# Moving a step's attention scores ahead of the next slot, and its Q and K transposes ahead of the previous step's values, in the transformer half of a Taylor-attention plus transformer kernel

## Chip, cores and metric

The kernel runs on one core of one Trainium2 chip. The metric is the device time of the whole kernel in microseconds (us). Engines: PE is TensorE (matmuls; PEld its weight loads), DVE is VectorE, ACT is ScalarE, POOL is GpSimd, SP is SyncE, which here only issues DMAs.

## What is computed

The input x is (8, 1024, 256), float32. It is layer-normalised to `xn`, and the result is `x + attention(xn) + ffn(xn)`:

```python
x = L0_attn_hidden_states
xn = _layernorm(x, axis=-1)
x = x + _L0_attn_ref(xn, ...) + _L0_ffn_ref(xn, ...)
```

The first branch is a linear attention with a Taylor feature map. The change doesn't touch it. The second branch is a transformer of two layers (DEPTH = 2) with 8 heads of 64, a local window of 128 tokens and a gated feed-forward part:

```python
h = shift_token(x)
q, k, v = jnp.split(h @ wqkv, 3, axis=-1)
q = l2norm(q) * qs; k = l2norm(k) * ksc
q, k = rotary_xpos(q, k)
o = local_attention(q, k, v)      # this block of 128 keys and the one before, masked softmax
x = x + o @ wo
h = shift_token(x)
h = (h - mu) / jnp.sqrt(var + 1e-05) * lg + lb
a, g = jnp.split(h @ w1 + b1, 2, axis=-1)
x = x + (a * gelu(g)) @ w2 + b2
```

## The kernel before, in words

`taylor_block` (lines up to 653) computes `xn` and the linear attention and leaves both in DRAM. Then `transformer_block` runs the two layers and adds everything up. All that follows is about `transformer_block`.

Work is cut into **steps**. A step is one tile of 128 tokens in one layer, `(n, s, l, it)`: its number n, the stream s (the batch is split into two streams), the layer l and the tile it of the stream. There are 4 x 32 = 128 steps. Time is cut into **slots**. In slot j every engine runs its own function `slot(nxt, cur, att, nrm, ffn)`, and five steps are in it at five stages:

- `nxt` (step of slot j+1): its input tile is transposed (`x_T`, lines 1319 and 1320) and copied to `hT` by ACT.
- `cur`: Q, K and V projections (`project`, line 1327, bank by bank), copies of K and Q to `qk` by ACT (line 1213), squares (1221), norms and rotation on DVE and POOL, and at the end of the slot the transposes of K and Q (`heads_T`, line 1332), which ACT copies to `kT` and `qT` (1235 and 1240).
- `att`: scores (`scores`, lines 1352 for the middle and 1359 for the corners of a band), mask and row maximum on DVE (1079, 1086), exponentials on ACT (1246), division on DVE (1096), transposes of the probabilities (`prob_T`, 1370 and 1374), the product with the values (`attend`, lines 1389 for the middle and 1399 for the corners), copy to `oT` by ACT (1259), and the output projection (`out_project`, 1408).
- `nrm`: residual add on DVE (`add_attention`, 1108), statistics (1113 and, of the shifted half `xsh`, 1115), reciprocal root on POOL (973), normalisation (1125, 1126), transposes (`hn_T`, 1415) and copy to `hnT` by DVE (1132).
- `ffn`: up projection and gate (`up`, 1431 and 1436), GELU on ACT (1268, 1271), product on DVE (1142), down projection (`down`, 1443), last add (1149 or 1155).

The order of the work is written out by hand: each engine's `slot` is a fixed list, the same in every slot, with semaphore waits between engines. An engine that waits holds up everything behind it. From slot 7 to slot 127 all five stages are filled, except that a few slots at the two ends miss one.

On DVE the list begins with `add_attention(nrm)`, which needs the output projection that is PE's last work of the slot before. Then come the four `mask_scores(att, p)`, the statistics, `normalise`, the rotations of K, the gate, the norm and rotations of Q, and `unit_k(cur)` (line 1069), which scales K by its norm and signals `k_unit`. `heads_T` of K waits for `k_unit`. Behind `unit_k` stand `add_ffn`, `set_mask(nxt)` and `copy_hnT(nrm)`.

On SP the list begins with `shift(nrm)` (lines 888 and 889), which waits for `x1_ready` of `add_attention` and moves half of the tile down by one row (`xsh`), for the second statistics. Behind it are `keep_k` (894), `carry` (914), `load_residual` (882, 883; it waits for `xb_ready` of POOL's `residual`, line 1007, and runs where l is 1), `place_v` (906, 907) and `keep_v` (899 to 901).

PSUM has 8 banks, and this table says who uses which:

```python
SCORES = (0, 1, 2, 3)
XT, HNT, K, V, Q, KT, QT, OT, WO, DOWN = 2, 3, 4, 5, 5, 4, 5, 0, 7, 6
UP = (6, 7, 4)
```

`prob_T` writes banks 0, 1 and 2 and `OT` takes two banks. Each sharing is guarded by a wait.

Of the kernel before, what the change touches and what calls it, by code (L numbers as in the profile page):

```python
# [669 lines left out]
def transformer_block(nc, PAIRS, x, xn_d, attn_d, wqkv_s, wo, w1, b1, w2, ln, qk_scale, rotary, masks, ident, out):  # L670
# [6 lines left out]
    with ExitStack() as ctx:  # L677
# [3 lines left out]
        def sem(name):  # L681
            return ctx.enter_context(nc.semaphore("f_" + name))
# [7 lines left out]
        ps = ctx.enter_context(nc.psum_tensor("f_ps", [P, 8, 512], F32))  # L690

        SCORES = (0, 1, 2, 3)
        XT, HNT, K, V, Q, KT, QT, OT, WO, DOWN = 2, 3, 4, 5, 5, 4, 5, 0, 7, 6
        UP = (6, 7, 4)

        wo_s = sb("fwo_s", [P, LAYERS, INNER // P, DIM])
# [65 lines left out]
        hT_ready = sem("hT_ready")  # L762
# [32 lines left out]
        pT_ready = sem("pT_ready")  # L795
# [3 lines left out]
        x1_ready = sem("x1_ready")  # L799
# [5 lines left out]
        hnT_ready = sem("hnT_ready")  # L805
# [4 lines left out]
        x2_ready = sem("x2_ready")  # L810
# [43 lines left out]
        def some(count):  # L854
            return not isinstance(count, int) or count > 0
# [340 lines left out]
        def _(act):  # L1196
# [33 lines left out]
            def copy_kT(step):  # L1230
                n, s, l, it = step
                if some(it):
                    act.wait_ge(k_kept[s][l], 16 * it)
                act.wait_ge(kT_ps, n + 1)
                a.activation(kT[s][l][:, :, P:2 * P], ps[:, KT, :].rearrange("p (c n) -> p c n", n=P), ACT.Copy).then_inc(kT_ready, 1)

            def copy_qT(step):
                n, s, l, it = step
                act.wait_ge(qT_ps, n + 1)
                a.activation(qT[:, :, :], ps[:, QT, :].rearrange("p (c n) -> p c n", n=P), ACT.Copy).then_inc(qT_ready, 1)  # L1240
# [35 lines left out]
            def slot(nxt, cur, att, nrm, ffn):  # L1276
                if att:
                    for p in range(3):
                        exps(att, p)
                if cur:  # L1280
                    copy_part(cur, 1, K, k_ps, k_ready)
                if att:
                    exps(att, 3)
                if cur:
                    square(cur, 1, k_ready, ssqk_sum, sqk_ready)
                    copy_part(cur, 0, Q, q_ps, q_ready)
                    square(cur, 0, q_ready, ssqq_sum, sqq_ready)
                if ffn:
                    gelus(ffn)
                if cur:  # L1290
                    copy_v(cur)
                if att:
                    copy_pT(att)
                if cur:
                    a.activation(primed_s[:, :], mhalf[:, 0:1], ACT.Exp)
                if att:
                    copy_oT(att)
                if cur:
                    copy_kT(cur)
                    copy_qT(cur)  # L1300
                if nxt:
                    copy_hT(nxt)

            run(act, slot, 3)

        @block.tensor
        def _(pe):
# [14 lines left out]
            def project(step, i, b, done):  # L1322
                n, s, l, it = step
                pe.wait_ge(hT_ready, n + 1)
                for c in range(KC):
                    rows = hT[s][l][:, 0:P] if c else hT[s][l][:, P + 1:2 * P + 1]
                    last = mm(ps[:, b, :], rows, wqkv_s[:, l, c, i * INNER:(i + 1) * INNER], start=(c == 0), stop=(c == KC - 1))  # L1327
                last.then_inc(done, 1)

            def heads_T(step, i, b, done):  # L1330
                for h in range(0, HEADS, 2):
                    last = tr(ps[:, b, h // 2 * P:(h // 2 + 1) * P],  # L1332
                              qk[:, i * HEADS + h:i * HEADS + h + 2, :].rearrange("p h d -> p (h d)"), id_s[:, :])
                last.then_inc(done, 1)

            def scores(step, cur, ffn, p):
                n, s, l, it = step
                if p == 0:
                    pe.wait_ge(kT_ready, n + 1)
                    pe.wait_ge(qT_ready, n + 1)  # L1340
                if p == 2 and cur:
                    pe.wait_ge(hT_ready, cur[0] + 1)
                if p == 2 and ffn:
                    pe.wait_ge(hnT_ready, ffn[0] + 1)
                for k in range(2):
                    middle, corner = k * 256 + k * HALF, k * 256 + (1 - k) * P
                    for q in (p, p + 1):
                        h = PAIRS_OF_HEADS[q][k]
                        r = slice(h % 2 * HD, h % 2 * HD + HD)
                        for half in range(2):  # L1350
                            rows = slice(half * HALF, half * HALF + HALF)
                            mm(ps[rows, SCORES[q], middle:middle + P], qT[r, h // 2, rows], kT[s][l][r, h // 2, HALF:HALF + P],  # L1352
                               start=True, stop=True)
                    for q in (p, p + 1):
                        h = PAIRS_OF_HEADS[q][k]
                        r = slice(h % 2 * HD, h % 2 * HD + HD)
                        for half in range(2):
                            rows = slice(half * HALF, half * HALF + HALF)
                            last = mm(ps[rows, SCORES[q], corner:corner + HALF], qT[r, h // 2, rows],  # L1359
                                      kT[s][l][r, h // 2, half * BAND:half * BAND + HALF], start=True, stop=True)  # L1360
                        if k == 1:
                            last.then_inc(score_ps, 1)
# [81 lines left out]
                last.then_inc(down_ps, 1)  # L1444

            def slot(nxt, cur, att, nrm, ffn):
                if att:
                    for p in (0, 2):
                        scores(att, cur, ffn, p)
                if cur:  # L1450
                    project(cur, 1, K, k_ps)
                    project(cur, 0, Q, q_ps)
                if ffn:
                    up(ffn, cur, nrm)
                if cur:
                    pe.wait_ge(q_ready, cur[0] + 1)
                    project(cur, 2, V, v_ps)
                if att:
                    prob_T(att)
                if ffn:  # L1460
                    down(ffn)
                if att:
                    if nrm and not ffn:
                        pe.wait_ge(x1_ready, nrm[0] + 1)
                    attend(att)
                if cur:
                    pe.wait_ge(k_unit, cur[0] + 1)
                    heads_T(cur, 1, KT, kT_ps)
                    pe.wait_ge(v_ready, cur[0] + 1)
                    pe.wait_ge(q_rotated, cur[0] + 1)  # L1470
                    heads_T(cur, 0, QT, qT_ps)
                if nxt:
                    x_T(nxt)
                if nrm:
                    hn_T(nrm)
                if att:
                    out_project(att)

            run(pe, slot, 2)


# [97 lines left out]
```

## Time and profile before

| | |
|---|---|
| three runs | 3824.41 us median, 3824.31 to 3825.34 |
| the profiled execution | 3827.29 us, its span 3825.5 us |
| granted TensorE clock, mean | 0.985 of full speed |
| PE busy | 3661.6 us (96%), 34784 matmuls |
| DVE busy | 2835.6 us (74%) |
| ACT busy | 2756.8 us (72%) |
| POOL busy | 1247.2 us (33%) |
| transformer part | from 1117.6 us of the span to its end |

In a timeline a line gives the start, the time taken by the merged group (xN instructions), the engine, the line of the code, and in brackets the idle time before it with what ended it. Instructions are pipelined, so that the next starts some 0.08 us (DVE) or 0.16 us (PE) before the row of the one ahead has ended; the time that a piece of work takes is best read from start to start. Matmul ends are modelled.

### The profile page before, as it was taken

To read this page: it belongs to the slowest core of one execution; us is meant where nothing else is said; L and a number is where in the kernel's file an instruction comes from. 1 tells how busy PE (TensorE), PEld (TensorE's weight loads), DVE (VectorE), ACT (ScalarE), POOL (GpSimd) and SP (SyncE) were. 2 spreads that over 40 slices of the span, in tenths; PEclk is the share of its full clock that TensorE was granted. 3 is DMA by queue.
4 is the path that set the end of the run, shared out by engine and by line. 5 is a ranking of instruction groups with operands and counts; after the bars stand their busy time and mean duration, and the time that the engine had idled before them with its cause. 6 is when DMAs were issued, how large, how long until landed. Compare 5 with 4: busy or idle time off the path is not lost.

```text
span 3825.5 us, 92479 instructions
## 1 busy us (share of the span) xinstructions
PE 3661.6 (96%) x34784; PEld 2549.4 (67%) x34784; DVE 2835.6 (74%) x8672; ACT 2756.8 (72%) x6076; POOL 1247.2 (33%) x1319
## 2 busy tenths in 40 slices
PE   7999999999958999999999999999999999999997
PEld 3434444443426777777777777777777777777776
DVE  5766776776655877877877877877878778778774
ACT  5687677768735777777777777777777777777774
POOL 2211221221123433333333333333334334333332
PEclk9999999999978999999999999999999999999999
DMA  2100100110031222222222222222222222222210
GB/s 80 35 24 13 35 24 13 34 35 13 13 119 47 54 68 63 57 68 63 57 68 62 57 68 60 59 68 62 57 64 64 60 64 61 63 63 59 66 49 24
DMA packets 213054, 202.04 MB, mean 53 GB/s; under 512 B 31744, under 2 KB 171264, under 8 KB 211968
## 3 DMA queue, kind: packets, MB, share of 16 engines
q1 hardware_dynamic: 212608, 196.12, 18.6%
q8 instruction: 277, 4.54, 0.5%
q14 instruction: 169, 1.38, 0.1%
HBM read 46.87 MB, written 25.17 MB: 19 GB/s over the span
## 4 chain that ended last, share of the span: by engine, by line
PE 44%; DVE 13%; issue 6%; SPq 3%; DMA 2%; POOL 1%; ACT 0%; DVEq 0%; POOLq 0%
PE f_ps L1327 11%; PE f_ps L1431 9%; PE f_ps L1443 5%; PE f_ps L1408 5%; DVE pr L1096 3%; PE f_ps L1332 3%; PE f_ps L1352 2%; PE f_ps L1389 2%; DVE cosine L1046 2%; PE f_ps L1370 2%; DMA xsh<-x 2%; DVE act_u L1142 2%; DVE ssq L1054 2%; PE f_ps L1399 1%; DVE pr L1079 1%
## 5 line engine op out<-in xcount | busy, mean ns | idle before, releaser
L1246 ACT ACTIVATE pr<-pr,nmax,rnorm 128x192 f32<-128x192 f32 x1024 | 545.9, 535 | 347.1 <-DVE nmax L1086 347.1
L1327 PE MATMUL f_ps<-wqkv_s,hT 128*128 128x512 f32 x1536 | 717.5, 603 | 10.9 <-ACT hT L1208 5.5
L488 ACT ACTIVATE weights<-t_ps,four_s 128x1024 f32<-128x1024 f32 (+3 forms) x768 | 630.5, 906 | 103.6 <-PE t_ps L593 98.7
L1431 PEld LDWEIGHTS f_ps<-hnT,w_s 128*128 128x128 f32 x5120 | 593.4, 192 | 60.4 <-issue 58.8
L1431 PE MATMUL f_ps<-hnT,w_s 128*128 128x128 f32 x5120 | 594.8, 276 | 0.8 <-DVE hnT L1132 0.8
L1096 DVE TENSOR_SCALAR pr<-pr,rsum 128x192 f32<-128x192 f32 x1024 | 450.2, 500 | 9.0
L1327 PEld LDWEIGHTS f_ps<-wqkv_s,hT 128*128 128x128 f32 x1536 | 272.5, 190 | 270.1 <-issue 246.0
L973 POOL TENSOR_TENSOR rstd<-ve,f_mhalf 128x1 f32<-128x1 f32 x128 | 81.5, 637 | 1121.6 <-DVE ve L1120 1121.6
L985 POOL TENSOR_TENSOR turned<-qk,rot 128x256 f32<-128x256 f32 x512 | 394.7, 795 | 57.5 <-ACT qk L1213 44.0
L392 DVE SCALAR_TENSOR_TENSOR weights<-weights,causal_s 128x512 f32<-128x512 f32 x256 | 210.9, 826 | 244.8 <-ACT weights L488 244.8
L1079 DVE CUSTOM_DVE_ANT_0 pr<-f_ps,mask 128x192 f32<-128x192 f32 x1024 | 326.3, 355 | 68.3 <-PE f_ps L1359 66.6
L593 PE MATMUL t_ps<-qkT 96*128 96x512 bf16 (+3 forms) x1536 | 345.0, 333 | 14.5 <-ACT weights L488 9.8
L607 PE MATMUL t_ps<-weights,vals 128*32 128x512 f32 (+3 forms) x3072 | 332.6, 506 | 26.7 <-DVE weights L392 20.2
L1443 PE MATMUL f_ps<-w_s,act_u 128*128 128x256 f32 x1536 | 354.3, 380 | 1.6 <-DVE act_u L1142 1.3
L999 POOL TENSOR_TENSOR rnorm<-ssq,f_mhalf 128x8 f32<-128x8 f32 x128 | 248.1, 1938 | 298.8 <-DVE ssq L1056 298.8
L593 PEld LDWEIGHTS t_ps<-qkT 96*128 96x128 bf16 x1536 | 107.5, 98 | 325.3 <-ACT weights L488 244.7
L1443 PEld LDWEIGHTS f_ps<-w_s,act_u 128*128 128x128 f32 x1536 | 281.9, 190 | 37.4 <-DVE act_u L1142 3.0
L270 POOL TENSOR_TENSOR yT<-yT,den 128x1024 f32<-128x1024 f32 x24 | 58.1, 2423 | 681.2 <-DVE den L319 681.2
L992 POOL TENSOR_TENSOR rnorm<-ssq,f_mhalf 128x8 f32<-128x8 f32 x128 | 210.6, 1645 | 198.3 <-DVE ssq L1056 198.3
L1132 DVE TENSOR_SCALAR hnT<-f_ps,ln_s 128x128 f32<-128x128 f32 x256 | 93.3, 405 | 227.8 <-PE f_ps L1415 227.8
L1259 ACT ACTIVATE oT<-f_ps 128x512 f32<-128x512 f32 x128 | 76.5, 598 | 252.1 <-PE f_ps L1399 252.1
L1408 PE MATMUL f_ps<-fwo_s,oT 128*128 128x256 f32 x1024 | 242.7, 380 | 1.9 <-ACT oT L1259 1.8
(132 smaller groups left out, 7070.3 us busy)
## 6 DMA issues: line engine op xcount, KB each, us to landing
vw<-vw SPq DMA_DIRECT2D x628, 128.0 KB, 2.4
kT<-kT SPq DMA_DIRECT2D x124, 256.0 KB, 2.6
xs<-x_dram SPq DMA_DIRECT2D x8, 1024.0 KB, 7.9
xn_dram<-xn SPq DMA_DIRECT2D x8, 1024.0 KB, 5.3
attn_dram<-ao SPq DMA_DIRECT2D x8, 1024.0 KB, 4.5
xin<-xn_dram SPq DMA_DIRECT2D x64, 128.0 KB, 2.2
xres<-x_dram SPq DMA_DIRECT2D x64, 128.0 KB, 2.0
xres<-attn_dram SPq DMA_DIRECT2D x64, 128.0 KB, 2.2
```

Source lines behind the costliest of these rows:

```text
L488: a.activation(weights[:, 2 * (u % UNITS):2 * (u % UNITS) + 2, c:512], ps[:, unit_bank(n):unit_bank(n) + 2, c:512], ACT.Square, bias=four_ ...
L593: last = mm(ps[:, unit_bank(n) + k, c:512], qkT[:, 1, place, j * P:(j + 1) * P], qkT[:, 0, place, half * 512 + c:(half + 1) * 512], start= ...
L607: last = mm(ps[h * VP:(h + 1) * VP, half, c:512], vals[:, j, g * GH + h, :], weights[:, 4 * i % (2 * UNITS) + h, c:512], start=(j == 0), s ...
L985: g.tensor_tensor(turned[:, heads, f], qk[:, heads, z], sines, ALU.mult).then_inc(done, 1)
L999: g.tensor_tensor(rnorm[:, :HEADS], ssq[:, :HEADS], mhalf[:, :HEADS], ALU.pow).then_inc(qnorm_ready, 1)
L1079: last = v.tensor_tensor_reduce(out=chances(h), in0=ps[:, SCORES[p], k * 256:k * 256 + BAND], in1=mask[s][l][:, HALF - k * HALF:HALF - k * ...
L1096: last = v.tensor_scalar_mul(chances(h), chances(h), rsum[:, h:h + 1])
L1246: last = a.activation(chances(h), chances(h), ACT.Exp, bias=nmax[:, h:h + 1], scale=rnorm[:, h:h + 1], accum_out=psum[:, h:h + 1])
L1327: last = mm(ps[:, b, :], rows, wqkv_s[:, l, c, i * INNER:(i + 1) * INNER], start=(c == 0), stop=(c == KC - 1))
L1408: last = mm(ps[:, WO, 0:DIM], oT[:, c, :], wo_s[:, l, c, :], start=(c == 0), stop=(c == INNER // P - 1))
L1431: last = mm(ps[:, UP[j // 2], o:o + P], w1_s[:, l, c, half * FULL + j * P:half * FULL + j * P + P], hnT[:, c, :], start=(c == 0), stop=(c ...
L1443: last = mm(ps[:, DOWN, 0:DIM], act_u[:, j, :], w2_s[:, l, j, :], start=(j == 0), stop=(j == FB - 1))
```

## The change

Three things are done. All are in `transformer_block`.

1. `scores` is called for `cur` at the end of its own slot, behind `attend(att)`, and no longer for `att` at the head of the next slot.
2. `heads_T` of K and of Q stand ahead of `attend(att)` and not behind it. ACT's list follows: `copy_kT` and `copy_qT` stand ahead of the small exponential that loads the table, and ahead of `copy_oT`.
3. The banks of `XT`, `HNT`, `OT` and `DOWN` are new, and the waits that guard them: the Q projection waits for `hnT_ready`, the third and fourth pair of scores for `x2_ready`.

DVE's, SP's and POOL's lists are not changed. A line of the PE's code has a number one smaller than before (1326 for 1327), and the small exponential is 1297 for 1295.

```diff
-        XT, HNT, K, V, Q, KT, QT, OT, WO, DOWN = 2, 3, 4, 5, 5, 4, 5, 0, 7, 6
+        XT, HNT, K, V, Q, KT, QT, OT, WO, DOWN = 4, 5, 4, 5, 5, 4, 5, 6, 7, 3
         UP = (6, 7, 4)
...
                 if att:
                     copy_pT(att)
                 if cur:
+                    copy_kT(cur)
+                    copy_qT(cur)
                     a.activation(primed_s[:, :], mhalf[:, 0:1], ACT.Exp)
                 if att:
                     copy_oT(att)
-                if cur:
-                    copy_kT(cur)
-                    copy_qT(cur)
...
-            def scores(step, cur, ffn, p):
+            def scores(step, att, ffn, p):
                 n, s, l, it = step
                 if p == 0:
                     pe.wait_ge(kT_ready, n + 1)
                     pe.wait_ge(qT_ready, n + 1)
-                if p == 2 and cur:
-                    pe.wait_ge(hT_ready, cur[0] + 1)
+                if p == 0 and not att and some(n):
+                    pe.wait_ge(pT_ready, 3 * n)
                 if p == 2 and ffn:
-                    pe.wait_ge(hnT_ready, ffn[0] + 1)
+                    pe.wait_ge(x2_ready, ffn[0] + 1)
...
             def slot(nxt, cur, att, nrm, ffn):
-                if att:
-                    for p in (0, 2):
-                        scores(att, cur, ffn, p)
                 if cur:
                     project(cur, 1, K, k_ps)
+                    if ffn:
+                        pe.wait_ge(hnT_ready, ffn[0] + 1)
                     project(cur, 0, Q, q_ps)
...
                 if ffn:
                     down(ffn)
-                if att:
-                    if nrm and not ffn:
-                        pe.wait_ge(x1_ready, nrm[0] + 1)
-                    attend(att)
                 if cur:
                     pe.wait_ge(k_unit, cur[0] + 1)
                     heads_T(cur, 1, KT, kT_ps)
                     pe.wait_ge(v_ready, cur[0] + 1)
                     pe.wait_ge(q_rotated, cur[0] + 1)
                     heads_T(cur, 0, QT, qT_ps)
+                if att:
+                    if nrm and not ffn:
+                        pe.wait_ge(x1_ready, nrm[0] + 1)
+                    attend(att)
+                if cur:
+                    for p in (0, 2):
+                        scores(cur, att, ffn, p)
                 if nxt:
                     x_T(nxt)
```

PE, the end of a full slot before, from the last matmul of `down` on; f_k_unit is what DVE's `unit_k` signals.

```order
L1443 MATMUL f_ps<-w_s,act_u 128x256 [waits f_u_ready] x6
L1389 MATMUL f_ps<-pT,vw 64x128 [waits f_pT_ready,f_v_placed11,f_v_ready]
L1399 MATMUL f_ps<-pT,vw 64x64 x15
L1332 MATMUL f_ps<-f_id,qk 128x128 [waits f_k_unit]
L1332 MATMUL f_ps<-f_id,qk 128x128 [waits f_q_rotated,f_v_ready]
L1319 MATMUL f_ps<-f_id,xmid 128x128 [waits f_x2_ready]
L1415 MATMUL f_ps<-f_id,hn 128x128 [waits f_hn_ready]
L1408 MATMUL f_ps<-fwo_s,oT 128x256 [waits f_oT_ready]
L1352 MATMUL f_ps<-kT,qT 64x128 [waits f_qT_ready,f_kT_ready]
L1327 MATMUL f_ps<-wqkv_s,hT 128x512 [waits f_hT_ready]
```

PE, the same place of the changed kernel.

```order
L1442 MATMUL f_ps<-w_s,act_u 128x256 [waits f_u_ready] x6
L1331 MATMUL f_ps<-f_id,qk 128x128 [waits f_k_unit]
L1331 MATMUL f_ps<-f_id,qk 128x128 [waits f_q_rotated,f_v_ready]
L1388 MATMUL f_ps<-pT,vw 64x128 [waits f_pT_ready,f_v_placed00,f_v_ready]
L1398 MATMUL f_ps<-pT,vw 64x64 x15
L1351 MATMUL f_ps<-kT,qT 64x128 [waits f_qT_ready,f_kT_ready]
L1351 MATMUL f_ps<-kT,qT 64x128 [waits f_x2_ready]
L1318 MATMUL f_ps<-f_id,xin 128x128 [waits f_xn_in1]
L1414 MATMUL f_ps<-f_id,hn 128x128 [waits f_hn_ready]
L1407 MATMUL f_ps<-fwo_s,oT 128x256 [waits f_oT_ready]
L1326 MATMUL f_ps<-wqkv_s,hT 128x512 [waits f_hT_ready]
```

The wait for f_k_unit now stands right behind `down`; `attend` (1388, 1398) and the scores (1351 and 1358) have come between it and the output projection (1407).

ACT, end of a full slot, as a piece of the difference.

```order
-L1295 ACTIVATE primed_s<-f_mhalf 128x1
-L1259 ACTIVATE oT<-f_ps 128x2x2x128 [waits f_oT_ps]
 L1235 ACTIVATE kT<-f_ps 128x4x128 [waits f_kT_ps,f_k_kept10]
 L1240 ACTIVATE qT<-f_ps 128x512 [waits f_qT_ps]
+L1297 ACT_TABLE_LOAD
+L1297 ACTIVATE primed_s<-f_mhalf 128x1
+L1259 ACTIVATE oT<-f_ps 128x2x2x128 [waits f_oT_ps]
 L1205 ACTIVATE hT<-hT,mask 128x1 [waits f_mask_set11]
```

The copies of K and Q come first, and the table load has moved from ahead of the copy to `oT`, where it stood behind `copy_pT`, to between them and it.

## Rows read from the trace of the kernel before

**Rows 1.** Windows: the stretch of full slots, busy time by engine, clock, DMA.
```profile
1240.00:3708.00 2468.00, 2462.39 (x25444) 1942.89 (x25439) 1955.55 (x6721) 1837.04 (x4560) 947.75 (x960) 1.00 0.24 62
```

**Rows 2.** Timeline of PE: K and Q projections that open slots 6, 7 and 127.
```profile
1222.36 3.70 PE L1327 MATMUL f_ps<-wqkv_s,hT 128*128 128x512 f32 x8
...
1240.12 3.70 PE L1327 MATMUL f_ps<-wqkv_s,hT 128*128 128x512 f32 x8
...
3708.31 3.70 PE L1327 MATMUL f_ps<-wqkv_s,hT 128*128 128x512 f32 x8
```

**Rows 3.** Timeline of PE: two neighbouring full slots.
```profile
2431.95 0.45 PE L1352 MATMUL f_ps<-kT,qT 64*64 64x128 f32 x8
...
2433.45 3.70 PE L1327 MATMUL f_ps<-wqkv_s,hT 128*128 128x512 f32 x8
...
2443.60 1.04 PE L1370 MATMUL f_ps<-f_id,pr 128*128 128x128 f32 x8
2447.60 1.09 PE L1389 MATMUL f_ps<-pT,vw 128*64 128x128 f32 x16
2449.25 1.09 PE L1332 MATMUL f_ps<-f_id,qk 128*128 128x128 f32 x8
2453.94 3.70 PE L1327 MATMUL f_ps<-wqkv_s,hT 128*128 128x512 f32 x8
```

**Rows 4.** Timeline of DVE, from the end of one slot to the end of the next.
```profile
2428.01 0.69 DVE L1069 TENSOR_TENSOR qk<-qk,rnorm 128x512 f32<-128x512 f32 x1
...
2432.13 0.42 DVE L1108 TENSOR_TENSOR x<-f_ps,xmid 128x256 f32<-128x256 f32 x1 [1.07 <-PE f_ps L1408]
2433.03 0.36 DVE L1079 CUSTOM_DVE_ANT_0 pr<-f_ps,mask 128x192 f32<-128x192 f32 x1 [0.48 <-PE f_ps L1359]
...
2436.53 0.29 DVE L1115 BATCH_NORM_STATS2 st<-xsh 128x6 f32<-128x128 f32 x1
...
2440.23 1.75 DVE L1096 TENSOR_SCALAR pr<-pr,rsum 128x192 f32<-128x192 f32 x4
...
2442.69 1.63 DVE L1142 SCALAR_TENSOR_TENSOR act_u<-f_ps,b_s,act_u 128x128 f32<-128x128 f32 x6
...
2447.35 0.69 DVE L1069 TENSOR_TENSOR qk<-qk,rnorm 128x512 f32<-128x512 f32 x1
```

**Rows 5.** Timeline of ACT: copies at a slot's end, and the table load ahead.
```profile
2425.01 1.28 ACT L1295 ACT_TABLE_LOAD   x1
...
2430.01 0.59 ACT L1240 ACTIVATE qT<-f_ps 128x512 f32<-128x512 f32 x1
```

**Rows 6.** Waits from 1300 to 3700: engine, line, for whom: us, times, longest.
```profile
DVE st L1115 <- DMA xsh<-x: 54.3, 58, 2.1
...
PE f_ps L1332 <- DVE qk L1069: 4.3, 17, 0.5
```

**Rows 7.** Timeline of SP: the queue ahead of a late shift.
```profile
2453.79 0.98 SPq L901 DMA_DIRECT2D vw<-vw  x1
2454.82 0.59 SPq L888 DMA_DIRECT2D xsh<-x  x1
```

**Rows 8.** Timeline of PE: first matmuls behind long waits, at either clock.
```profile
1136.43 1.97 PE L1332 MATMUL f_ps<-f_id,qk 128*128 128x128 f32 x8 [4.75 <-DVE qk L1069]
...
1228.70 3.23 PE L1327 MATMUL f_ps<-wqkv_s,hT 128*128 128x512 f32 x4 [2.65 <-ACT qk L1213]
```

**Rows 9.** Windows of PE alone: busy, clock, DMA, around two waits.
```profile
1228.60:1231.80 3.20, 3.10 (x5) 0.61 0.00 0
182.00:186.00 4.00, 3.73 (x58) 1.00 0.70 237
```

**Rows 10.** Timeline of PE: the 1.83 us wait of the second window.
```profile
182.12 3.30 PE L572 MATMUL t_ps<-t_idb,parts 128*96 128x128 bf16 x56 [1.83 <-issue]
```

**Rows 11.** DVE line 1096 from 1400 to 3600: ns min/median/max, and mean by group.
```profile
L1096 DVE TENSOR_SCALAR pr<-pr,rsum x856: 304/320/871, 1408.4 to 3593.3; 128x192 f32<-128x192 f32 x172
...
L1096 DVE TENSOR_SCALAR pr<-pr,rsum 128x192 f32<-128x192 f32 x856 | 382.9, 507 | 7.5
```

## The prediction

> **What bounds the kernel now.** I read the busy times by stretch first, since the change touches the transformer part alone. In the full slots PE is busy 2462.4 of 2468 us at the full clock, which is the 2.4 GHz level; DVE is busy 1955.6 and ACT 1837.0 [rows 1]. The reader would call it bound by PE. Next comes the length of a slot: 120 slots lie between the projections at 1240.12 and 3708.31, so a slot takes 20.57 us [rows 2], and an undisturbed one 2453.94 - 2433.45 = 20.49 us [rows 3]. So PE loses 0.08 us a slot to waits, and no order of its work, which stays the same, can win more than 120 x 0.08 = 10 us.
>
> Then I looked for what comes close behind PE. There is a **loop** through DVE. I call the end of `unit_k` U. PE transposes K and Q, then x and hn, projects the output, and DVE adds: from U = 2428.01 + 0.69 = 2428.70 to 2432.13 this takes 3.43 us. From the add to the first mask it is 0.90 us, of which 0.48 is a wait for the scores. From the first mask at 2433.03 to the next U at 2447.35 + 0.69 = 2448.04 DVE works 15.01 us with no gap for another engine [rows 4]. The loop is 3.43 + 0.90 + 15.01 = 19.34 us, against PE's 20.49: a slack of 1.15 us, after which `unit_k` hardly ever keeps PE waiting (17 times, 4.3 us) [rows 6]. A check on the loop: slot 6 has no feed-forward part, so DVE saves the gate, which is some 1.6 us [rows 4], and the loop should take about 17.75 us; the slot took 1240.12 - 1222.36 = 17.76 us [rows 2].
>
> **The change, part by part.** No instruction is added or removed; what moves are waits.
>
> *K and Q transposed ahead of the values.* DVE's list is the same, so U doesn't come earlier for it. `attend` used to lie ahead of the wait for U and covered it; now it lies behind. Its step is 2449.25 - 2447.60 = 1.65 us [rows 3], and it enters the loop whole, since `out_project` needs it. Loop +1.65.
>
> *Scores in their own slot.* They stood behind the output projection and so ran beside DVE's add. Now they stand ahead of it: 2433.45 - 2431.95 = 1.50 us [rows 3], which enter the loop too. In return DVE no longer waits for scores. Behind the add the mask can start at once, and by pipelining the step of an add with a busy time of 0.42 us is some 0.35 us, so 0.90 becomes 0.35. Loop +1.50 - 0.55.
>
> New loop: 19.34 + 1.65 + 1.50 - 0.55 = **21.94 us**. That is 1.45 us above PE's 20.49, and PE stands idle for as long in front of line 1331, in every slot.
>
> *What else is in those waits.* `qT` is ready at 2430.01 + 0.59 = U + 1.90 [rows 5]; the scores start at U + 0.06 + 0.93 + 1.65 = U + 2.6, so `attend` hides both copies. The table load of 1.28 us [rows 5] and the small exponential of 0.2 us now follow, then `oT`: 1.90 + 1.5 + 0.6 = U + 4.0, while the output projection comes at U + 4.6. Nobody waits. The probabilities: DVE's last division ends at 2440.23 + 1.75 = 2441.98, 8.95 us behind the mask [rows 4], and PE comes to their transposes 10.15 us behind the K projection [rows 3]. In the new order the projection starts about 0.5 us ahead of the mask, so PE arrives 0.7 us late enough, and doesn't wait. The new waits of the Q projection for `hnT` and of the scores for `x2` cost nothing: DVE does the last add right behind `unit_k`, and `copy_hnT` ends near U + 5.8, the Q projection comes at U + 8. The banks cost and give nothing by themselves.
>
> *SP.* Its list is the same. Before, DVE waits for the shifted half in about every other slot, 54.3 us over 58 times or 0.94 us each [rows 6]: the seven DMAs ahead of the shift are issued until 2453.79 + 0.98 = 2454.77, which is U + 6.7, and the shift at 2454.82 comes late [rows 7]. Now the add ends at U + 3.43 + 3.15 + 0.42 = U + 7.0, so the queue is just free. But the second statistics also ask 0.55 us sooner, at 0.35 + (2436.53 - 2433.03) = 3.85 us behind the add instead of 4.40 [rows 4]. I can't tell what is left: nothing if the shift lands as in slots without the burst, 0.94 as before. I take 0.35 us in every other slot, 0.17 a slot, for the queue is free but the DMAs of the burst are still under way.
>
> *The sum.* 21.94 + 0.17 - 20.57 = +1.54 us a slot, over 120 slots 185 us. The two slots before the full ones gain 1.7 and 2.6 by the same loop (their slack is already gone), the drain at the end nothing: it holds the same chain. Together +189 us, that is 3827.3 + 189 = 4016 us against the profiled execution, and 2.9 less against the median of the runs shown: **4013 us**.
>
> The smallest value: no DMA wait and 0.1 us a slot less by pipelining, 1.37 x 120 - 12 + 4 = +156, so 3980. The largest: the old wait of 0.94 us in every other slot, 0.47 a slot, makes (1.37 + 0.47) x 120 + 4 = +225, so 4049, and 10 us for a wait at the probabilities, which had 0.7 us to spare: 4060.
>
> **Rivals.**
>
> *The clock falls (0.06).* A wait of 1.45 us in every slot could cost the full clock. Behind a wait of 2.65 us the first matmuls of the V projection took 3.23 us for four [rows 8], with 0.61 of the clock granted in that stretch, much of it at the 1.2 GHz level [rows 9]; behind one of 1.83 us the clock stayed at 1.00 and 56 transposes took 3.30 us [rows 9, 10]. So 1.45 us looks safe, but here it is followed by transposes and small tiles only. At the low level the eight transposes of K and Q take 1.97 us [rows 8] for 1.09 [rows 3]. That is 0.88 us a slot at least, and about as much for `attend`: 1.7 x 120 = 204 us more, near 4215. By the Trainium skill (TensorE: Matmul & The Clock Gate, section on PSUM-queue cycling) short idles between groups of matmuls, which cycle through PSUM banks, can make the clock swing between its levels; the full slots before show 1.00 with their few short waits, so the trace does not bear it out here.
>
> *PE stays the bound and the time stays (0.04).* PE is the busiest by far and its work is unchanged; if the loop were not closed by `add_attention` but had slack somewhere, the slot would stay at 20.57 us and the time near 3824. Against it: the loop explains slot 6 to 0.1 us. By the Trainium skill (Perfetto Trace Analysis, section Identifying the Most-Contended Engine) the engine of the highest occupancy is the one to optimise first; a reader who judges the change by that alone gets this case.
>
> *DVE's stretch shrinks, no slower or slightly faster (0.04).* The divisions of line 1096 take 320 ns in the median but 507 in the mean, up to 871 [rows 11], where POOL's rotations run beside them. If in the new order POOL's work fell elsewhere, eight of them would save 8 x 0.187 = 1.50 us, the loop would be 20.44, PE's 20.49 would bind again, and the remaining waits of 0.08 us a slot would go: 3824.4 - 10 = 3815 us. It decides from the point at which the mask-to-U stretch falls below 20.57 - 6.93 = 13.6 us. Against it: POOL starts behind DVE's own variance, so the two keep their places to each other.
>
> **How the numbers follow.** The loop case has 0.86 and gives 3980 to 4060 us, with 4013 as its middle. The clock case has 0.06 and lies above; the other two have 0.08 and lie below. Leaving them out leaves 0.14, so the range is that of the loop case. A measurement of this kernel tells 0.2% (8 us) from no change. Faster by that: 0.04. Within: 0.04. Slower: 0.92.
>
> **What would show it.** In the new profile the slot is about 22 us. PE waits for DVE at line 1331 once a slot, 1.2 to 1.6 us, and 150 to 190 us in all. DVE's wait at line 1079 for the scores (0.48 us) is gone, its stretch from the first mask to U is still near 15 us, and its wait for `xsh` is smaller. The clock of the full slots stays at 1.00. I am wrong if the wait at 1331 is under 0.5 us, if DVE's stretch is under 14, or if another wait of PE (1369 or 1351) is among the large ones.

## The result and the profile after

The changed kernel takes **4009.0 us** (median of four runs, 4006.2 to 4014.5) against 3824.4 us of the kernel before: the ratio is 1.048, 95% interval 1.047 to 1.050. Its profiled execution took 4014.5 us, with a span of 4012.7 us.

The stretch of full slots, by window (us; busy PE, PEld, DVE, ACT, POOL; clock; DMA share; GB/s). It answers to [rows 1].

```profile
1250.00:3890.00 2640.00, 2449.41 (x25444) 1944.53 (x25443) 1937.34 (x6727) 1825.46 (x4560) 927.19 (x960) 1.00 0.22 58
```

No engine is busy for longer than before: the same 25444 matmuls take 2449 us instead of 2462. But the stretch is 172 us longer, and now no engine fills it: PE is at 93%, DVE at 73%, ACT at 69%. PE's timeline, the projections that open slots 7, 8 and 127, as in [rows 2]:

```profile
1249.66 3.60 PE L1326 MATMUL f_ps<-wqkv_s,hT 128*128 128x512 f32 x8
...
1271.46 3.60 PE L1326 MATMUL f_ps<-wqkv_s,hT 128*128 128x512 f32 x8
...
3888.56 3.60 PE L1326 MATMUL f_ps<-wqkv_s,hT 128*128 128x512 f32 x8
```

A slot takes (3888.56 - 1249.66) / 120 = 21.99 us, where it took 20.57. One slot on PE:

```profile
2427.75 2.75 PE L1442 MATMUL f_ps<-w_s,act_u 128*128 128x256 f32 x12
2432.05 1.09 PE L1331 MATMUL f_ps<-f_id,qk 128*128 128x128 f32 x8 [1.54 <-DVE qk L1069]
2433.07 1.09 PE L1388 MATMUL f_ps<-pT,vw 128*64 128x128 f32 x16
2434.10 0.69 PE L1398 MATMUL f_ps<-pT,vw 64*64 64x64 f32 x32
2434.61 0.40 PE L1351 MATMUL f_ps<-kT,qT 64*64 64x128 f32 x8
...
2436.56 1.89 PE L1407 MATMUL f_ps<-fwo_s,oT 128*128 128x256 f32 x8
2438.29 3.60 PE L1326 MATMUL f_ps<-wqkv_s,hT 128*128 128x512 f32 x8
```

`down` is done, and PE stands for 1.54 us until `unit_k` is ready. Behind it come, back to back, the transposes, the values, the scores and the output projection. DVE in the same slot, to be read beside [rows 4]:

```profile
2431.31 0.69 DVE L1069 TENSOR_TENSOR qk<-qk,rnorm 128x512 f32<-128x512 f32 x1
...
2438.56 0.43 DVE L1108 TENSOR_TENSOR x<-f_ps,xmid 128x256 f32<-128x256 f32 x1 [1.07 <-PE f_ps L1407]
2438.90 0.35 DVE L1079 CUSTOM_DVE_ANT_0 pr<-f_ps,mask 128x192 f32<-128x192 f32 x1
...
2453.18 0.69 DVE L1069 TENSOR_TENSOR qk<-qk,rnorm 128x512 f32<-128x512 f32 x1
```

From U = 2432.00 to the add 6.56 us, from there to the mask 0.34, from the mask to the next U = 2453.87 it is 14.97: together 21.87 us. The waits, from 1300 to 3880 (us in total, times, longest), against [rows 6]:

```profile
DVE hnT L1132 <- PE f_ps L1414: 499.2, 117, 5.8
...
PE f_ps L1331 <- DVE qk L1069: 185.0, 117, 1.9
...
DVE st L1115 <- DMA xsh<-x: 2.9, 5, 0.9
```

PE waits 1.58 us a slot for DVE, and DVE waits 4.3 us a slot for PE, at another place. Each is idle while the other works, which is what a closed loop looks like. The wait at line 1331 is also nearly all that PE stands idle for: from 1300 to 3880 it is busy for 2393.96 of 2580 us, which leaves 186.0, of which this wait is 185.0. The wait for the shifted half has gone from 54.3 to 2.9 us.

**Where the 187 us lie.** In the profiled executions, 170.7 us are in the 120 slots from 7 to 127 (2638.9 against 2468.2), 9.5 us ahead of them and 7.0 us behind. Of the 9.5, slot 6 has 2.6 (1249.66 - 1229.29 = 20.37 us, against 17.76) and 2.1 us are there before the first projection of the part (1125.85 against 1123.77). These 2.1 us are scatter: the code ahead of the part is the same in all the kernels here, and the part starts anywhere between 1113.0 and 1119.7 us in their profiled executions.

### The profile page after: what moved, and what is told of

Read it like the earlier page. It is cut to its first block, busy times and chain, and to the rows that moved or that the text cites. A ratio compares the mean times of both kernels' runs of the same rounds, so it can differ in the third digit from the quotient of the medians.

```text
span 4012.7 us, 92480 instructions
## 1 busy us (share of the span) xinstructions
PE 3652.5 (91%) x34784; PEld 2551.6 (64%) x34784; DVE 2815.5 (70%) x8672; ACT 2745.9 (68%) x6076; POOL 1226.8 (31%) x1319
## 4 chain that ended last, share of the span: by engine, by line
DVE 38%; PE 20%; issue 11%; DMA 1%; SPq 1%; ACT 1%; POOL 1%; DVEq 0%; POOLq 0%; ACTq 0%
DVE pr L1096 9%; DVE pr L1079 6%; PE f_ps L1407 5%; DVE act_u L1142 4%; DVE cosine L1046 4%; DVE ssq L1054 4%; PE f_ps L1331 3%; PE f_ps L1388 3%; PE f_ps L1351 3%; DVE qk L1069 2%; DVE qk L1063 2%; PE f_ps L1398 2%; PE f_ps L1358 1%; DVE hn L1125 1%; DVE hn L1126 1%
## 5 line engine op out<-in xcount | busy, mean ns | idle before, releaser
L1326 PE MATMUL f_ps<-wqkv_s,hT 128*128 128x512 f32 x1536 | 706.0, 596 | 12.2 <-ACT qk L1213 6.5
L1096 DVE TENSOR_SCALAR pr<-pr,rsum 128x192 f32<-128x192 f32 x1024 | 471.9, 521 | 9.0
L1326 PEld LDWEIGHTS f_ps<-wqkv_s,hT 128*128 128x128 f32 x1536 | 283.2, 191 | 270.5 <-issue 246.9
L985 POOL TENSOR_TENSOR turned<-qk,rot 128x256 f32<-128x256 f32 x512 | 373.9, 752 | 89.3 <-ACT qk L1213 76.3
L1235 ACT ACTIVATE kT<-f_ps 128x512 f32<-128x512 f32 x128 | 76.5, 597 | 420.2 <-PE f_ps L1331 420.2
L1331 PE MATMUL f_ps<-f_id,qk 128*128 128x128 f32 x1024 | 143.4, 284 | 214.0 <-DVE qk L1069 214.0
L1331 PEld LDWEIGHTS f_ps<-f_id,qk 128*128 128x128 f32 x1024 | 112.5, 143 | 266.9 <-DVE qk L1069 266.9
```

What stands on the lines that cost most here:

```text
L985: g.tensor_tensor(turned[:, heads, f], qk[:, heads, z], sines, ALU.mult).then_inc(done, 1)
L1096: last = v.tensor_scalar_mul(chances(h), chances(h), rsum[:, h:h + 1])
L1331: last = tr(ps[:, b, h // 2 * P:(h // 2 + 1) * P], qk[:, i * HEADS + h:i * HEADS + h + 2, :].rearrange("p h d -> p (h d)"), id_s[:, :])
```

## Experiments

Beside total times I give the slot cut in three, as the mean of 41 to 49 slots between 1300 and 2300 us, worked out from the starts in DVE's timeline (U is the end of line 1069, `unit_k`):

| kernel | time, us | slot | U to add | add to mask | mask to U |
|---|---|---|---|---|---|
| before | 3824.4 | 20.58 | 4.09 | 0.88 | 15.60 |
| changed | 4009.0 | 22.04 | 6.66 | 0.34 | 15.04 |
| e1, banks | 3829.4 | 20.55 | 4.12 | 0.89 | 15.55 |
| e2, transposes first | 4005.8 | 22.01 | 6.07 | 0.89 | 15.05 |
| e3, e2 with the table early | 3955.9 | 21.62 | 5.64 | 0.89 | 15.10 |
| e4, scores only | 3952.9 | 21.50 | 6.09 | 0.34 | 15.07 |
| e5, before + 1 reduction | 3856.3 | 20.88 | 3.70 | 0.90 | 16.28 |
| e6, before + 3 | 3948.6 | 21.55 | 3.44 | 0.89 | 17.22 |
| e10, before + 6 | 4255.8 | 23.90 | 4.40 | 0.90 | 18.59 |
| e12, changed + half | 4114.1 | 23.04 | 7.36 | 0.35 | 15.34 |
| e7, changed + 1 | 4244.4 | 23.86 | 7.91 | 0.35 | 15.61 |
| e8, changed, norm late | 3941.9 | 21.47 | 6.58 | 0.34 | 14.54 |
| e9, changed, norm and statistics late | 3916.0 | 21.30 | 6.59 | 0.34 | 14.37 |
| e11, before, statistics later | 3818.1 | 20.49 | 4.65 | 0.89 | 14.95 |

Each was timed in turn with the kernel before on the same chip (medians of that one 3822.6 to 3824.9); the intervals of the ratios are within 0.0018 either way.

**The theory** is that of the prediction: PE and DVE hold each other in a loop, which had a slack of about 1 us a slot; the two moved pieces of PE work take it up and more. The rivals: the banks; the work of one move alone; PE's own pipelining; the clock.

### e1: the banks alone

```diff
-        XT, HNT, K, V, Q, KT, QT, OT, WO, DOWN = 2, 3, 4, 5, 5, 4, 5, 0, 7, 6
+        XT, HNT, K, V, Q, KT, QT, OT, WO, DOWN = 2, 1, 4, 5, 5, 4, 5, 6, 7, 3
...
-                if p == 2 and ffn:
+                if p == 0 and ffn:
                     pe.wait_ge(hnT_ready, ffn[0] + 1)
+                if p == 2 and some((ffn or nrm or step)[0]):
+                    pe.wait_ge(x2_ready, (ffn or nrm or step)[0])
```

> The kernel before in its old order, with only PSUM banks dealt anew (OT 6, DOWN 3, HNT 1) and the waits that go with them. Loop theory (the change is slow because two pieces of PE work entered the chain through DVE, and banks cost nothing by themselves): no change, 3824 us, within 8. Rival (the new banks make engines wait for each other): a good part of the 185 us, so 3870 or more, with new waits at line 1352 or 1443.

Measured: 3829.4 us, ratio 1.0013 (1.0004 to 1.0022). Some 5 us more, and not in the full slots (20.55 us each). The moves of `OT` and `DOWN` don't explain the 185 us. `XT` and `HNT` can't take the changed kernel's places in the old order without further waits, since the transposes of K and Q use the same banks just ahead; those two were not tried alone. In the changed kernel's trace PE has no wait beside line 1331 but two at line 1442, 0.8 us together, so no wait of PE is left that they could have made.

### e2 and e3: the transposes ahead of attend

e2 is the kernel before with two edits of the change; the scores and banks stay.

```diff
 # PE
-                if att:
-                    ...
-                    attend(att)
                 if cur:
                     ...
                     heads_T(cur, 0, QT, qT_ps)
+                if att:
+                    ...
+                    attend(att)
 # ACT
+                if cur:
+                    copy_kT(cur)
+                    copy_qT(cur)
                     a.activation(primed_s[:, :], mhalf[:, 0:1], ACT.Exp)
                 if att:
                     copy_oT(att)
-                if cur:
-                    copy_kT(cur)
-                    copy_qT(cur)
```

> The kernel before with only the K and Q transposes ahead of attend, and ACT's new list (copies of K and Q, table load, then oT); scores stay at the head of the next slot, banks stay. Loop theory: attend adds 1.65 us to the chain, and since the scores no longer stand between the transposes and the output projection, oT (ready 4.0 us behind the end of unit_k) comes 0.95 us later than PE (3.1 us behind it). Loop 19.34 + 1.65 + 0.95 = 21.94 us a slot, about 3990 us, with a new wait of PE at line 1408 for ACT of some 0.9 us a slot. Rival (costs are separate, and ACT's list is covered): 20.99 a slot, 3875 us, and no wait at 1408.

Measured: 4005.8 us, 16 us above the forecast; the slot is 22.01 us, not 21.94, which is half of these 16, and the other half lies outside the full slots. This half of the change costs nearly as much as the whole. ACT's timeline in one slot, and the same moment on PE:

```profile
2428.50 0.59 ACT L1240 ACTIVATE qT<-f_ps 128x512 f32<-128x512 f32 x1
2429.11 1.28 ACT L1297 ACT_TABLE_LOAD   x1
2430.41 0.20 ACT L1297 ACTIVATE primed_s<-f_mhalf 128x1 f32<-128x1 f32 x1
2430.52 0.58 ACT L1259 ACTIVATE oT<-f_ps 128x512 f32<-128x512 f32 x1
```
```profile
2426.98 1.09 PE L1331 MATMUL f_ps<-f_id,qk 128*128 128x128 f32 x8 [0.40 <-DVE qk L1069]
...
2429.93 0.38 PE L1414 MATMUL f_ps<-f_id,hn 128*128 128x128 f32 x2
2431.15 1.99 PE L1407 MATMUL f_ps<-fwo_s,oT 128*128 128x256 f32 x8 [0.84 <-ACT oT L1259]
```

The values were done at about 2429.7, but ACT is loading its table until 2430.4, so PE waits 0.84 us for `oT`. In the changed kernel the scores stand in this place, and PE doesn't wait for `oT`.

e3 moves only the table:

```diff
                 if cur:
+                    a.activation(primed_s[:, :], mhalf[:, 0:1], ACT.Exp)
                     copy_kT(cur)
                     copy_qT(cur)
-                    a.activation(primed_s[:, :], mhalf[:, 0:1], ACT.Exp)
```

> As the run before it, but ACT loads its table ahead of the copies of K and Q, where it has time. Loop theory: oT is then ready 0.5 us after PE would like it, at 3.5 us behind unit_k, so the loop is 19.34 + 1.65 + 0.4 = 21.4 us and the time about 3925 us. Rival (ACT's list is covered anyway): the same time as the run before it.

Measured: 3955.9 us, 50 us less. The rival of both runs, that ACT's list is covered anyway, falls. The forecast was 31 us too low: the slot is 21.62 and not 21.4, 0.16 of it between U and the add, and 0.1 in DVE's stretch.

### e4: the scores in their own slot, the transposes where they were

```diff
 # the changed kernel, with attend(att) again ahead of heads_T(cur, ...), and on ACT:
+                if cur:
+                    a.activation(primed_s[:, :], mhalf[:, 0:1], ACT.Exp)
+                if att:
+                    copy_oT(att)
                 if cur:
                     copy_kT(cur)
                     copy_qT(cur)
-                    a.activation(primed_s[:, :], mhalf[:, 0:1], ACT.Exp)
-                if att:
-                    copy_oT(att)
```

> The changed kernel with attend again ahead of the K and Q transposes, and ACT's old list: only the scores and the banks are moved. Loop theory: the scores put 1.50 us into the chain and take 0.55 out of DVE's wait; attend no longer covers the copy of Q, so PE waits some 0.95 us for qT at line 1351. Loop 19.34 + 1.50 - 0.55 + 0.95 = 21.24 us, about 3915 us. Rival (moving the scores is the whole cost of the change): 3990 us or more. Rival (the scores are free, all of the cost is the transposes): 3830 us.

Measured: 3952.9 us. PE, two places in a slot:

```profile
2444.07 1.09 PE L1332 MATMUL f_ps<-f_id,qk 128*128 128x128 f32 x8 [0.25 <-DVE qk L1069]
2446.06 0.45 PE L1352 MATMUL f_ps<-kT,qT 64*64 64x128 f32 x8 [0.89 <-ACT qT L1240]
```

The scores right behind the transposes wait 0.89 us for the copy of Q, as reckoned. The forecast was 38 us too low: from U to the add it takes 6.09 us and not 5.88, and DVE's stretch 15.07 and not 15.01, together some 32 us; the rest lies outside the full slots and was not followed. Both one-sided rivals fall: neither move is free and neither is the whole.

The two halves cost 181 and 128 us, and together 185. That is no contradiction: each half alone opens a wait (for `oT`, for `qT`) which the other half covers. The loop gives all three; a sum of separate costs gives none.

### e5 and e6: is there a slack in the kernel before?

```diff
                 if cur:
+                    for i in range(1):     # 3 in e6, 6 in e10
+                        v.reduce_sum(extra[:, i, :], cosine[:, HEADS:, :], AX)
                     unit_k(cur)
```

> The kernel before with one more reduction on DVE (0.61 us, result unused) ahead of unit_k. Loop theory: the chain has a slack of 1.15 us in undisturbed slots and about 0.2 us in the slots with a late shift, so at most the latter pay, 0.4 us each: 3824 to 3850 us. Rival (the kernel before is already bound through DVE, the slack is not there): 0.61 x 124 = 76 us more, 3900.

> The same with three reductions, 1.83 us. Loop theory: the slack of 1.15 is used up and the rest is paid: 19.34 + 1.83 = 21.17 us a slot without DMA waits, up to 22.1 in the slots with the late shift; 3895 to 3950 us. Rival (DVE has time enough, it is busy for 74% only): still 3824. Rival (already bound): 3824 + 227 = 4050.

Measured: 3856.3 and 3948.6 us. One reduction of 0.61 us costs 32 us and not 76; a little over the expected range. Slots whose statistics wait for a late shift take 21.2 us on PE, from projection to projection (1300 to 2300), where they took 20.66 in the kernel before; the others take 20.49 in both. Only the former pay, 0.5 of the 0.61 us, and those with slack pay nothing. Three reductions lengthen the stretch to 17.22 us and the slot to 21.55, which is the sum 17.22 + 0.89 + 3.44. The time is at the upper edge of the range. PE's wait in e6 (1300 to 3700) shows that the loop is closed here too:

```profile
PE f_ps L1335 <- DVE qk L1070: 104.8, 112, 1.7
```

### e8 and e9: shorten the stretch of the changed kernel

```diff
 # e8, DVE                                    # e9: row_statistics(nrm) too, right behind unit_k,
-                if nrm:                      # layer_norm(nrm) behind set_mask(nxt), and on POOL
-                    layer_norm(nrm)          # ln_root(nrm) behind norm_q(cur)
...
                 if cur:
                     unit_k(cur)
+                if nrm:
+                    layer_norm(nrm)
```

> The changed kernel with layer_norm moved on DVE from ahead of the Q rotation to right behind unit_k; its result is wanted 3 us later. Loop theory: the chain gets shorter by the 0.52 us of these two instructions, a slot takes 21.45 us, and the time falls by 0.52 x 124 = 64 us to 3945. Rival (the wait at 1331 isn't what sets the slot): no change, 4009.

Measured: 3941.9 us, 67 us less (expected 64). Not an instruction was removed, only moved to where DVE is idle anyway. This is the most direct sign that the loop through the wait at 1331 sets the slot.

> The changed kernel with both row_statistics and layer_norm moved on DVE behind unit_k, and POOL's reciprocal root behind its norm of Q. The five instructions of row_statistics take a step of 0.94 us, the two of layer_norm 0.52. Loop theory: the stretch falls from 15.04 to 13.6 us, the loop from 22.04 to 20.58, close to PE's own 20.49, and nearly all of the loss goes: 3820 to 3845 us, with PE waiting under 0.3 us a slot at 1331. Rival (the new order costs PE something of its own): a loss over the kernel before of 30 us or more stays.

Measured: 3916.0 us; it was expected at 3820 to 3845. The stretch went to 14.37 and not 13.6. DVE's waits from 1300 to 3700 tell why:

```profile
DVE cosine L1046 <- ACT qk L1213: 31.9, 105, 0.7
DVE rsum L1093 <- ACT pr L1246: 28.8, 112, 0.3
```

With the statistics away DVE comes to its divisions before ACT has done the exponentials and copied K: 0.54 us a slot are lost to two new waits, of the 0.77 that the stretch is longer than forecast; the other 0.2 are open. The next engine in the loop is ACT. A loss of 92 us remains, over the 30 of the rival (that the order costs PE something of its own). But the rival isn't its cause: from 1300 to 3700 PE is busy for 2294.62 of 2400 us, and the 105.4 us that are left are its waits at line 1331. A matmul takes PE 96.2 ns in the mean here (2294.62 us for 23842) and 96.8 in the kernel before (2394.39 us for 24729), so the new order costs PE nothing of its own, in pipelining or clock.

### e7, e10 and e12: what a longer wait costs

> The changed kernel with one such reduction. Loop theory: there is no slack left, so all of it is paid, 0.61 x 124 = 76 us over the changed kernel: 4085 us. Rival (PE's own order costs the time, in pipelining or clock, and the wait at 1331 only shows it): less than half of it, under 4045.

Measured: **4244.4 us**, 235 us over the changed kernel, where 76 were expected; neither theory had that. The stretch of DVE grew as it should (15.61). But from U to the add it takes 7.91 us and not 6.6. PE in two neighbouring slots, then the granted clock by windows of 10 us (busy PE; clock; DMA):

```profile
2410.99 1.42 PE L1334 MATMUL f_ps<-f_id,qk 128*128 128x128 f32 x8 [2.11 <-DVE qk L1070]
2412.34 1.98 PE L1391 MATMUL f_ps<-pT,vw 128*64 128x128 f32 x16
...
2435.36 1.87 PE L1334 MATMUL f_ps<-f_id,qk 128*128 128x128 f32 x8 [2.47 <-DVE qk L1070]
2437.16 1.93 PE L1391 MATMUL f_ps<-pT,vw 128*64 128x128 f32 x16
```
```profile
2400.00:2410.00 10.00, 8.88 (x58) 1.00 0.00 1
2410.00:2420.00 10.00, 9.01 (x135) 0.83 0.36 95
2420.00:2430.00 10.00, 10.00 (x65) 1.00 0.16 47
```

Behind a wait of 2.1 to 2.5 us the transposes took up to 1.97 us for 1.09, the values 1.98 for 1.09: the clock had fallen to the 1.2 GHz level, and came back by the projections. These matmuls are in the loop, so nearly every slot pays. It is the prediction's clock rival, one reduction away from the changed kernel, and near the size of 1.7 us a slot that was given to it: from U to the add a slot loses up to 1.9 us, 1.3 in the mean. With the longer stretch the slot is 1.82 us longer than in the changed kernel, which is 218 of the 235 us over 120 slots.

> The kernel before with six reductions of 0.61 us ahead of unit_k. Question: is it the length of PE's wait that takes the clock down (in the changed kernel with one reduction it fell at waits of 2.1 to 2.5 us), or the small matmuls that follow it in the new order. The loop without any loss of clock is 15.05 + 3.66 + 0.89 + 3.43 = 23.03 us, a wait of 2.5 us a slot, and the time 3824 + 2.46 x 122 = 4124 us, up to 4140. Theory of the wait alone: the clock falls as it did there, the eight transposes behind the wait take 1.9 us for 1.09, part of the output projection is slow as well, and the time is 4220 us or more. Rival (it takes the small matmuls): 4124 to 4140 us at a clock of 0.98.

Measured: 4255.8 us, at a clock of 0.96 in the full slots. In the old order, too, the clock falls: behind waits of 2.2 to 2.7 us the eight transposes took more than 1.18 us in 25 of 41 slots, and the output projection behind them was slow in 24 of 40. So it doesn't take the values and scores behind the wait: in this order transposes and the output projection follow. But it doesn't happen every time, though these waits are the longest of all runs. A slow row, with the granted clock at 0.59 from 2396 to 2400, and one at full speed:

```profile
2395.66 1.82 PE L1335 MATMUL f_ps<-f_id,qk 128*128 128x128 f32 x8 [2.30 <-DVE qk L1070]
...
2420.20 1.09 PE L1335 MATMUL f_ps<-f_id,qk 128*128 128x128 f32 x8 [2.31 <-DVE qk L1070]
```

> The changed kernel with a reduction over half the data ahead of unit_k, 0.34 us. In the changed kernel PE's waits at 1331 are 1.43 to 1.89 us and the transposes behind each of them took 1.09 us; with the whole reduction they are 2.03 us and more, and behind over half of them the transposes took more than 1.1 us, up to 1.97. Theory (the clock is kept below some 2 us and lost by chance above): the waits are now mostly 1.85 us, a few over 2, so the 0.34 us are paid nearly alone: 4009 + 0.34 x 122 = 4050 us, up to 4070, with a clock of 0.98 in the mean. Rival (the loss of clock grows in proportion with the wait): 4125 us, half of what the whole reduction cost.

Measured: 4114.1 us, near the rival's 4125. My limit of 2 us was read from the wrong row. The transposes behind the wait are at full speed nearly always, but the matmuls after them are not (PE, one slot; then the window with it, of which the last four numbers are POOL's, the clock, DMA share and GB/s):

```profile
2410.78 1.09 PE L1334 MATMUL f_ps<-f_id,qk 128*128 128x128 f32 x8 [1.84 <-DVE qk L1070]
2411.80 1.87 PE L1391 MATMUL f_ps<-pT,vw 128*64 128x128 f32 x16
```
```profile
2410.00:2414.00 4.00, 3.22 (x40) 2.73 (x43) 1.26 (x4) 2.44 (x4) 2.71 (x3) 0.74 0.05 11
```

Counted over the full slots by the sixteen matmuls of line 1391 (1388), slow is more than 1.18 us: in e8, with waits of 0.9 to 1.4 us, 0 of 116; in the changed kernel, waits of 1.43 to 1.90 us, 3 of 118; in e12, waits of 1.76 to 2.22 us, 45 of 108; in e7, 97 of 112. One of the three of the changed kernel:

```profile
1374.93 1.10 PE L1331 MATMUL f_ps<-f_id,qk 128*128 128x128 f32 x8 [1.89 <-DVE qk L1069]
1375.95 1.80 PE L1388 MATMUL f_ps<-pT,vw 128*64 128x128 f32 x16
```

In the changed kernel all three had waits of 1.85 to 1.90 us, as nine slots did; in e12 it is 17 of 45 slots with such waits, about the same share. The loss is neither proportional nor a step: in this order it goes from never below 1.7 us of wait to nearly always above 2.0. The length isn't all of it: in e10, in the old order, waits of 2.2 us and more slowed the transposes in some 60% of the slots. Whether the order makes this difference, or the moment at which the wait falls, no run here separates.

### e11: a version that is faster than both

```diff
 # the kernel before, DVE
-                if nrm:
-                    row_statistics(nrm)
                 if att:
                     normalise(att, 0)
+                if nrm:
+                    row_statistics(nrm)
```

> The kernel before with row_statistics on DVE moved behind the first four divisions, so that the shifted half has 2.2 us more to land. Loop theory: DVE's wait for xsh (1.0 us in every other slot) goes, all slots have their slack of 1.15 us, PE's rare waits at 1332 go, and a slot takes 20.49 us instead of 20.575: 3814 us, 10 us less. Rival (POOL's rotation, which starts behind the variance, comes later and makes DVE wait at line 1063, or beside other work of DVE): 3824 or more.

Measured: **3818.1 us** (11 runs), ratio to the kernel before 0.998, 0.997 to 0.999: 7 us less than the 3824.9 measured beside it, where 10 were expected. It is a small gain, but clear of the noise. The slot is 20.49 us, and from 1300 to 3700 PE has no idle time left that the profile shows:

```profile
1300.00:3700.00 2400.00, 2400.00 (x24815) 1895.51 (x24814) 1888.15 (x6568) 1794.95 (x4457) 946.55 (x935) 1.00 0.24 62
```

That is the end of this road: in this order PE's work leaves nothing to win in the full slots. Its 20.49 us hang a little on the order, though: in the changed kernel PE's work without the wait is 21.99 - 1.58 = 20.41 us a slot.

## Why the prediction was right

The forecast was 4013 us, the result 4009. Step by step:

- *The loop, 21.94 us.* Measured 21.87 in an undisturbed slot (6.56 + 0.34 + 14.97), against 6.58 + 0.35 + 15.01 in the sum. Slot 6, which the prediction gained 2.6 us for, took 20.37 us against 17.76. e8 shortens the loop and the time follows, e6 lengthens it past its slack and the time follows, e2 and e4 show each term in its place.
- *`attend` +1.65, scores +1.50, DVE's wait -0.55.* Right to 0.03 us together. One by one they are less exact: in the slot shown `attend` takes 1.54 us and the scores 1.45, and the rest of the way from U to the add 3.57 where it was 3.43; these misses nearly cancel. That the changed kernel has no wait for `qT` and `oT` was right too, and it isn't chance: e2 and e4 show what each wait costs (0.84 and 0.89 us) when its cover is gone.
- *SP and the shifted half, +0.17.* Mis-sized. The burst was out of the way, as expected: in the changed kernel it is issued until 2459.62 + 0.60 = 2460.22, the add ends at 2460.88 and the shift is issued at 2460.91. No more was needed: the wait fell from 0.94 us to next to nothing, 2.9 us in all. That term made the sum 20 us too high; half a microsecond less for the shift to land did no harm.

```profile
2459.62 0.60 SPq L901 DMA_DIRECT2D vw<-vw  x1
2460.91 0.54 SPq L888 DMA_DIRECT2D xsh<-x  x1
```

- *The edges, +4.* Mis-sized the other way: 16.5 us, or 14.4 without the scatter of 2.1 us ahead of the part. I had the 2.6 of slot 6 and gave slot 5 1.7, where it paid 0.7. In the drain I expected nothing and it paid 7.0. Near the start one cause can be read: in slot 3, which has no projections, the scores used to stand between the transposes of hn and `up`, and `up` now waits 0.82 us for DVE's copy. In the drain this wait of 0.82 us comes three times, where the kernel before has it once. I didn't follow the drain slot by slot, so how its 7 us divide is open.
- *The rest of the full slots.* The mean is 21.99 against 21.87: DVE's stretch varies (15.04 in the mean), and three slots lose some 1.55 us each to the clock. So the full slots cost 171 us where I had 185, and the edges 16.5 where I had 4. These two misses, 14 us too high and 12 too low, nearly cancel: that the forecast is only 4 us off is partly luck. (Among profiled executions it was 4016 against 4014.5. The medians stand 2.6 us closer together than these, since the profiled execution lies 5.5 us above the median in the changed kernel and 2.9 us in the one before.)
- *The check on slot 6.* It was weaker than it looked. In the kernel before U is there at 1235.38, and PE comes from the corners of `attend` (1234.77) to the transposes (1235.44) in 0.67 us, where a slot without any wait takes 0.63 (2448.62 to 2449.25). So PE's own path, with its wait of 2.65 us for ACT [rows 8], was as long as the loop to 0.04 us, and the 17.76 us fit either. That the loop sets slot 6 is shown by the changed kernel, where PE waits 1.99 us for `unit_k` in it.

The rivals: that PE stays the bound is refuted by the 185 us at line 1331. That rule of the occupancy (the Trainium skill, Perfetto Trace Analysis, Identifying the Most-Contended Engine) is given there with a caution: TensorE's headroom is to be judged by its weight loads and not by its busy matmuls. By the matmuls PE is the right engine before, at 99.8%; by the weight loads it is at 79% (1942.89 of 2468 us), no more than DVE (1955.55) [rows 1]. Neither number tells how far behind the next loop is, and an edit that gives PE no work still cost 5%. DVE's stretch didn't shrink (15.04; its divisions take 530 ns in the mean after, 507 before), as argued from POOL's tie to DVE. The clock rival came in 3 slots of 118, worth some 5 us, but was nearer than its 0.06 says: 45 in 108 with 0.34 us more. The Trainium skill's remark that short idles between groups of matmuls can make the clock swing (TensorE: Matmul & The Clock Gate, on PSUM-queue cycling) agrees in its effect with e7, e10 and e12, whose windows show 0.83, 0.59 and 0.74 behind such waits; here it is one wait a slot, for another engine.

## What to carry to other kernels

When one engine is busy for 99% look for the loop that comes second, and write down its length: the difference is the slack, and any piece of the busy engine's work that is moved to between "the other engine is done" and "the other engine can begin" is paid in full once the slack is gone. Such a piece may also be the cover of somebody else's wait (a copy, a table load), so halves of a reordering don't add up. And a wait that returns in every slot has a second price: here, from about 1.8 us of wait on, matmuls behind it ran at half clock in some slots and at 2.1 us in most, inside the same loop.

## What the runs showed of the hardware

- TensorE's clock fell behind single waits of about 1.8 us and more, in some slots and not in others, in an otherwise dense stretch: 0 of 116 slots with waits up to 1.4 us (e8), 3 of 118 with 1.43 to 1.90 (changed kernel), 45 of 108 with 1.76 to 2.22, mostly 1.85 (e12), 97 of 112 with 2.03 to 2.5 (e7), but only 25 of 41 with 2.2 to 2.7 in the old order (e10). It could fall with a delay: the eight transposes behind a wait of 1.84 us took 1.09 us, full speed, and the sixteen matmuls behind them 1.87 for 1.09. Yet in the linear-attention part a wait of 1.83 us was followed by 56 matmuls at full speed [rows 9, 10]: the length of one wait alone doesn't tell.
- A DVE stretch lengthened by 0.34 us cost 105 us (e12), by 0.61 us 235 us (e7), over some 122 slots; by the loop alone it would be 41 and 74.
